# A graph-attention layer on one core: s of the last two pairs of row tiles taken first, the first row of R made on chip, and the check of value ranges made later

## The reference

```python
Wh = X @ W.T
s_i = Wh @ r[:256, 0]
s_j = Wh @ r[256:, 0]
e = s_i[:, None] + s_j[None, :]
e = jnp.where(e >= 0, e, 0.2 * e)
e = jnp.where(A == 0, -jnp.inf, e)
output = jax.nn.softmax(e, axis=1) @ Wh
x = _layernorm(x + gelu(output), axis=-1)
```

## Time and profile before

| | |
|---|---|
| median of 3 runs | 1580.56 us (1579.71 to 1581.5) |
| profiled execution, own time | 1579.36 us |
| its span, first to last instruction | 1577.7 us |
| PE busy | 98% |
| DVE busy | 94% |
| ACT busy | 75% |
| POOL busy | 29% |
| mean granted TensorE clock | 0.992 of 2.4 GHz |

### The profile page before, as it was taken

The page is one execution under the profiler, slowest core; times in us unless marked ns, Lnnn a source line. Parts: engine busy times, 40 slices in busy tenths (PEclk is TensorE's granted clock), DMA queues, the critical chain, the costliest instruction groups (busy, mean ns, idle before and its releaser), DMA issues.

```text
span 1577.7 us, 37073 instructions
## 1 busy us (share of the span) xinstructions
PE 1545.3 (98%) x12685; PEld 1534.9 (97%) x12685; DVE 1483.0 (94%) x1852; ACT 1178.4 (75%) x1527; POOL 455.1 (29%) x660
## 2 busy tenths in 40 slices
PE   8969999999999999999999999999999999999995
PEld 7869999999999999999999999999999999999995
DVE  4789999999999999999999999999999999999995
ACT  5666687777777777877777777777777777777773
POOL 0022223232232323223332322333232233333220
PEclk9989999999999999999999999999999999999998
DMA  7466776968787696878778686877878687787860
GB/s 172 103 92 84 104 104 84 136 79 124 97 118 102 88 131 84 124 92 124 96 95 125 90 122 87 127 94 100 119 95 124 81 127 97 101 115 100 113 93 28
DMA packets 295267, 164.41 MB, mean 104 GB/s; under 512 B 12336, under 2 KB 291120, under 8 KB 295216
## 3 DMA queue, kind: packets, MB, share of 16 engines
q0 software_dynamic: 278976, 142.12, 68.9%
q1 hardware_dynamic: 16240, 21.80, 5.0%
HBM read 289.67 MB, written 8.42 MB: 189 GB/s over the span
## 4 chain that ended last, share of the span: by engine, by line
PE 95%; issue 3%; ACT 1%; DMA 1%; POOL 0%; SPq 0%; POOLq 0%; DVE 0%; ACTq 0%
PE acc L644 30%; PE acc L634 30%; PE acc L637 30%; PE acc L607 3%; PE acc L595 1%; ACT gates L338 0%; DMA Pw<-in_x 0%; DMA R_row<-w_rows 0%; ACT WV_hi L332 0%; ACT P_hi L414 0%; DMA w_rows<-w_in 0%; POOL adj_in L246 0%; POOL rstd L283 0%; SPq L191 0%; POOLq L58 0%
## 5 line engine op out<-in xcount | busy, mean ns | idle before, releaser
L634 PE MATMUL acc<-WV_hi,P_hi 128*128 (+1 forms) x4096 | 999.2, 282 | 8.2 <-ACT P_hi L414 8.1
L637 PE MATMUL acc<-WV_lo,P_hi 128*128 (+1 forms) x4096 | 998.1, 281 | 0.0
L634 PEld LDWEIGHTS acc<-WV_hi,P_hi 128*128 128x128 f32 x4096 | 775.1, 189 | 8.7 <-ACT P_hi L414 8.3
L414 ACT CAST P_hi<-Pw 128x1024 fp32r<-128x1024 f32 x512 | 536.5, 1048 | 317.5 <-DVE Pw L496 160.7
L637 PEld LDWEIGHTS acc<-WV_lo,P_hi 128*128 128x128 f32 x4096 | 772.9, 189 | 0.0
L496 DVE SCALAR_TENSOR_TENSOR Pw<-R_row,X,gatesT 128x512 f32<-128x512 f32 x1024 | 710.3, 746 | 2.6 <-DMA R_row<-w_rows 2.6
L506 DVE TENSOR_TENSOR P_lo<-Pw,P_hi 128x1024 fp32r<-128x1024 f32 x512 | 625.0, 1221 | 40.2 <-ACT P_hi L414 37.4
L246 POOL DMA_DIRECT2D adj_in<-in_adj x512 | 330.4, 654 | 873.5 <-ACT gates L338 819.1
L644 PE MATMUL acc<-WV_hi,P_lo 128*128 (+1 forms) x4096 | 576.2, 283 | 0.0
L338 ACT ACTIVATE gates<-adj_in 128x1024 uint8<-128x1024 bf16 x512 | 536.7, 1048 | 34.6 <-DMA adj_in<-in_adj 25.7
L644 PEld LDWEIGHTS acc<-WV_hi,P_lo 128*128 128x128 f32 x4096 | 527.5, 189 | 0.0
(11 more groups left out here) (60 smaller groups left out, 193.7 us busy)
## 6 DMA issues: line engine op xcount, KB each, us to landing
adj_in<-in_adj POOLq DMA_DIRECT2D x512, 256.0 KB, 5.3
out<-y SPq DMA_DIRECT2D x64, 128.0 KB, 6.0
y<-in_x POOLq DMA_DIRECT2D x60, 128.0 KB, 6.0
Pw<-in_x SPq DMA_DIRECT2D x48, 128.0 KB, 3.7
R_row<-w_rows SPq DMA_DIRECT2D x16, 256.0 KB, 6.6
x_res<-in_x SPq DMA_DIRECT2D x20, 128.0 KB, 2.7
w_in<-in_L_gnn_W SPq DMA_DIRECT2D x1, 256.0 KB, 2.7
w_rows<-w_in SPq DMA_DIRECT2D x1, 32.0 KB, 2.1
```

The costliest lines, as they stand in the source:

```text
L414: nc.scalar.copy(P_hi[:, u % 2], Pw[u][:]).then_inc(s_hi, 1)
L634: nc.tensor.matmul(acc[r_][:, v, 0:HC], P_hi[:, u % 2, par, bass.ts(v, P)], WV_hi[:, k, :], start=(first and u == 0 and par == 0), stop=False)
L637: nc.tensor.matmul(acc[r_][:, v, 0:FOUT], P_hi[:, u % 2, par, bass.ts(v, P)], WV_lo[:, k, :], start=False, stop=False)
```

## The change

1. PE runs `wh_product` only for pairs 0 to 29. For pairs 30 and 31 it first takes the two columns of s alone (`s_product`), then the 256 columns (`late_product`), after all of s is done. `copy_x(31)` goes between the two high parts of pair 29 on ACT.
2. The row 0 of R no longer goes through the memory. DVE multiplies an identity of 32 x 32 by the 16 columns of s that belong to the row (`spread`), one matmul with a matrix of ones puts the sum on all partitions (`ps_row`), DVE cuts it and ACT takes the exponential into `R_row[:, 0]`. The way through w_rows stays for the other rows.
3. The gates of pieces 0 and 1 are made on ACT during pairs 12, 14, ... 26; their loads are issued earlier, those of pieces 2 and 3 during the product, and the transpose of piece 0's gates goes behind pair 27 on DVE.
4. The high parts, low parts and maxima of tiles 60 to 63, and the second and third of the local extrema, move behind the start: on ACT two high parts into the first two groups, on DVE as `late_part` into pieces 1 to 5 of block 0, whose pieces are now written out.
5. The verdict goes to POOL (`verdict`), behind the adjacency loads of block 0. `applies` runs its body at once and waits for the flag at its end, with no branch on it.

```diff
         def applies(eng, body):
+            body()
             eng.wait_ge(s_flag, 1)
-            flag = eng.value_load(taken[0:1, 0:1], min_val=0, max_val=1)
-            with eng.If(flag == 1):
-                body()
...
-            load_rows(0, 0)
-
-            sp.wait_ge(s_Rld[0], 16)
...
+            pool.wait_ge(s_xT, 6)
+            load(0, 0, 0, 0)
             pool.wait_ge(s_xT, 10)
-            load(0, 0, 0, 0)
-            pool.wait_ge(s_xT, 18)
             load(0, 0, 0, 1)
-            pool.wait_ge(s_red, 2)
-            nc.gpsimd.partition_all_reduce(top[:, 0:2], red[:, 0:2], P, REDUCE_MAX).then_inc(s_top, 1)
-            pool.wait_ge(s_red, 3)
-            nc.gpsimd.partition_all_reduce(top[:, 2:3], red[:, 2:3], P, REDUCE_MAX).then_inc(s_top, 1)
+            pool.wait_ge(s_gate, GP)
+            load(0, 0, 1, 0)
+            pool.wait_ge(s_gate, 2 * GP)
+            load(0, 0, 1, 1)
+            pool.wait_ge(s_red, 1)
+            nc.gpsimd.partition_all_reduce(top[:, 0:1], red[:, 0:1], P, REDUCE_MAX).then_inc(s_top, 1)
...
+                def verdict():
+
+                    pool.wait_ge(s_red, 3)
+                    nc.gpsimd.partition_all_reduce(top[:, 1:3], red[:, 1:3], P, REDUCE_MAX).then_inc(s_fit, 1)
+                    pool.wait_ge(s_fit, 1)
+                    nc.gpsimd.tensor_scalar(fits[:, 0:1], top[:, 0:1], top[:, 1:2], MAX_SPREAD, ALU.add, ALU.is_le).then_inc(s_fit, 1)
+                    nc.gpsimd.tensor_scalar(fits[:, 1:3], top[:, 0:2], MAX_S, None, ALU.is_le).then_inc(s_fit, 1)
+                    nc.gpsimd.tensor_scalar(fits[:, 3:4], top[:, 2:3], MAX_WH, None, ALU.is_le).then_inc(s_fit, 1)
+                    pool.wait_ge(s_fit, 4)
+                    for q in range(1, 4):
+                        nc.gpsimd.tensor_tensor(fits[:, 0:1], fits[:, 0:1], fits[:, q:q + 1], ALU.mult).then_inc(s_fit, 1)
+                        pool.wait_ge(s_fit, 4 + q)
+                    nc.gpsimd.tensor_copy(taken[0:1, 0:1], fits[0:1, 0:1]).then_inc(s_flag, 1)
...
+            act.wait_ge(s_rcut, 1)
+            nc.scalar.activation(R_row[:, 0, :], R_row[:, 0, :], ACT.Exp, bias=shift[:], scale=ALPHA - 1.0).then_inc(s_R0, 1)
             act.wait_ge(s_cut, 1)
             nc.scalar.activation(Rc[:].rearrange("p (r m) -> p m r", r=4),
                                  s_i_cut[:].rearrange("p (m r) -> p m r", r=4),
                                  ACT.Exp, bias=shift[:], scale=ALPHA - 1.0).then_inc(s_Rc, 1)
-            nc.scalar.activation(X[:], S[:, :, 1], ACT.Exp, bias=shift[:], scale=1.0 - ALPHA)
+            act.wait_ge(s_wh, NP - 1)
+            late_high_part(NC - 4)
+            late_high_part(NC - 3)
             act.wait_ge(s_Rt, 1)
...
                             nc.scalar.copy(P_hi[:, u % 2], Pw[u][:]).then_inc(s_hi, 1)
+                            if not before and c == 0 and u < 2:
+                                if u == 0:
+                                    act.wait_ge(s_wh, NP)
+                                late_high_part(NC - 2 + u)
...
+            low_part_of(2 * (NP - 3))
+            copy_s(NP - 3)
+            copy_late_s(NP - 2)
+            dve.wait_ge(s_s, NP - 1)
+            row_s = S[0:32, :, 0].rearrange("p (g e) -> p g e", e=4)[:, :, 0:1]
+            nc.vector.tensor_tensor(spread, ident[0:32, 0:32].unsqueeze(1).to_broadcast([32, 16, 32]),
+                                    row_s.to_broadcast([32, 16, 32]), ALU.mult).then_inc(s_dg, 1)
+            copy_late_s(NP - 1)
             dve.wait_ge(s_s, NP)
             nc.vector.tensor_reduce(red[:, 0:1], S[:, :, 1], AX.X, ALU.max).then_inc(s_red, 1)
-            nc.vector.tensor_reduce(red[:, 1:2], S[:, :, 1], AX.X, ALU.min, negate=True).then_inc(s_red, 1)
+            low_part_of(2 * (NP - 3) + 1)
+            wh_maximum(NP - 3)
             dve.wait_ge(s_top, 1)
...
             dve.wait_ge(s_dve, 2)
+            dve.wait_ge(s_row, 1)
+            nc.vector.tensor_scalar(R_row[:, 0, :], ps_row, neg_M[:], None, ALU.max).then_inc(s_rcut, 1)
...
+            def late_part(n):
+
+                if 1 <= n <= 4:
+                    low_part_of(NC - 5 + n)
+                if n == 2 or n == 4:
+                    wh_maximum(NP - 3 + n // 2)
+                if n == 5:
...
-            for j in range(NP):
+            for j in range(NP - 2):
                 wh_product(j)
...
+            s_product(NP - 2)
+            s_product(NP - 1)
+            pe.wait_ge(s_dg, 1)
+            pe.wait_ge(s_const, 3)
+            nc.tensor.matmul(ps_row, ones, spread.rearrange("p g n -> p (g n)"), start=True, stop=True).then_inc(s_row, 1)
+            late_product(NP - 2, 0)
+            late_product(NP - 2, 1).then_inc(s_wh, 1)
+            late_product(NP - 1, 0)
             pe.wait_ge(s_Rc, 1)
-            nc.tensor.transpose(acc[0][0:NC, 0, 0:P], Rc[:], ident[:]).then_inc(s_Rt, 1)
+            nc.tensor.transpose(ps_Rt, Rc[:], ident[:]).then_inc(s_Rt, 1)
+            late_product(NP - 1, 1).then_inc(s_wh, 1)
```

More of the change, by code:

```diff
@@ L109, in narrow_path @@
         ps_wh = [half[:, :, 0:FOUT + 2] for half in (acc[1][:, 0:2], acc[1][:, 2:4], acc[0][:, 2:4])]
+        ones = y[0:32, 0, 0:P]
+        spread = y[0:32, 2:4, :].rearrange("p u (g n) -> p (u g) n", n=32)
+        ps_s = [acc[0][:, j, 0:4] for j in range(2)]
+        ps_row = acc[0][:, 0, :]
+        ps_Rt = acc[0][0:NC, 1, 0:P]
         gate_of = gatesT[:].bitcast(U8).rearrange("p b (i r) -> p b r i", r=4)
@@ L134, in narrow_path @@
         s_flag = sem("flag_ready")
+        s_X = sem("x_factors_ready")
         s_Rc = sem("r_columns_ready")
@@ L298, in block_loads @@
                             scale_bias(t - 1)
-                block_loads(0, 0, first=2, before=False)
+                def verdict():
[10 more added lines that the diff above has]
+                    nc.gpsimd.tensor_copy(taken[0:1, 0:1], fits[0:1, 0:1]).then_inc(s_flag, 1)
+                block_loads(0, 0, first=4, before=False)
+                verdict()
                 block_loads(0, 1)
@@ L322, in copy_x, with high_part @@
                 nc.scalar.copy(xT[:, j % 2, :], ps_xT[j % 2]).then_inc(s_xTc, 1)
-            def high_part(j):
+            def high_part(j, between=None):
                 act.wait_ge(s_wh, j + 1)
@@ L333, in high_part @@
                                          scale=V[:, k:k + 1]).then_inc(s_hi0, 1)
+                    if between and r_ == 0:
+                        between()
             def gate(i, u):
@@ L398, in row_block @@
                     for c in range(PC):
-                        ahead = not (last and c == PC - 1)
+                        ahead = not (last and c == PC - 1) and (before or c > 0)
                         if ahead:
                             act.wait_ge(s_adj[1 - c % 2], 64 * (PC // 2 * t + c // 2) + 64 * (1 + c % 2))
-                            if before or c > 0:
-                                act.wait_ge(s_mask, PC * t + c)
+                            act.wait_ge(s_mask, PC * t + c)
                         for u in range(GP):
@@ L507, in low_part, with piece @@
                                             ALU.subtract).then_inc(s_lo, 1)
-                def piece(ah, r_, cp, i, first=False, den_of=None):
+                def piece(ah, r_, cp, i, first=False, den_of=None, late=False):
                     t = 2 * ah + r_
@@ L521, in piece @@
                             low_part(GP * n + (u - 1), u - 1)
+                        if late and u == 1:
+                            late_part(2 * cp + i)
                         if den_of is not None and u == 1:
@@ L532, in row_block @@
                     e = t - 1 if before else None
-                    dve.wait_ge(s_Rld[r_], 16 * ah + 16)
-                    piece(ah, r_, 0, 0, first=not before, den_of=e)
+                    if not before:
+                        dve.wait_ge(s_R0, 1)
+                        for n in range(PC):
+                            piece(ah, r_, n // 2, n % 2, first=n == 0, late=True)
+                        return
+                    dve.wait_ge(s_Rld[r_], 16 * ah + 16 * r_)
+                    piece(ah, r_, 0, 0, den_of=e)
                     piece(ah, r_, 0, 1)
```

102 lines of the change are left out of this document (66 added, 36 removed).

## The result

The changed kernel takes 1587.02 us (median of 4 runs, 1585.18 to 1590.04), the kernel before 1580.84 in the same set. The ratio is 1.0045, 95% interval 1.0031 to 1.0058: slower by 6.2 us by the medians and 7 by the ratio, where 9 us faster was forecast. On another chip the same kernel gave 1.0023 (1.0011 to 1.0036). The profiled execution has 1585.18 us with a span of 1583.5.

What follows compares the result with a forecast made beforehand. PE was taken to bound the kernel, with a hole of 12.15 us and a half clock before the main part to win. Start 7.7 plus clock 2.6 minus waits 1.3 made 9.0 us: 1580.56 to 1571.6 us, range 1570.0 to 1575.5.

Steps and rivals of the forecast that it cites:

- Seven steps at 0.73 and a reduction are some 5.5 us ... free: Verdict on POOL behind block 0's last load: some 5.5 us, delaying block 1's first load by about 2.5, at no cost.
- a slack of 3.9 us: Block 1's first load: wanted 12 us after the end of piece 5, needs 8.1, which leaves 3.9.
- The prediction's own worst case: Verdict on POOL at 1.4 us a step: it would cost up to 1 us.
- POOL's loads of pieces 2 and 3 are issued before 76 and cost nothing: POOL's adjacency loads during the x product, issued before 76 us: no cost to the start.
- the 7.7 us forecast for the start: Start of the main part: first matmul moves from 92.10 to 84.4 us, 7.7 earlier; range 6.2 to 7.9.
- The clock: Rival: clock falls in the pause before the main part (1572.9 us) or already in the thin stretch (1574.0); chance 0.20.
- the thin stretch: PE's sparse work from 76.3 us: s products, ones, late products; a clock drop there puts the start at about 86.8.
- I expect the full clock throughout: PE around the main part's start: no pause over 1 us, so the half clock's cost of 2.6 us is won.
- Late work on DVE: Block 0, pieces 1 to 5: 3.7 us of late work gives 1.3 us of PE waits; bounds 0 and 3.7.
- The rival on the slower side: Clock drops in the thin stretch and stays at half well into block 0; at six groups 1590 us; chance 0.02.
- colliding x loads: Rival: adjacency loads collide with streaming x, PE waits in some pairs; 1579.6 us, no measurable change; chance 0.03.

Runs made afterwards that it cites:

- e2: The changed kernel with the verdict's comparisons and flag on DVE in piece 7 of block 0, the reduction still on POOL: 1574.61 us, ratio 0.9959.
- e5: The changed kernel again, unchanged, for a second profile: 1581.51 us, ratio 1.0023.
- e11: The kernel of e1 with DVE waiting in piece 5 for the verdict's flag, so at rest during the verdict: 1580.0 us in its one run.
- e6: The kernel of e1 with the first load of row block 1 issued ahead of the verdict, which stays on POOL: 1572.0 us, ratio 0.9962.
- e4: The kernel before, with piece 1's four loads issued behind the transposes of pair 31 instead of pair 17: 1584.35 us, ratio 1.0034.
- e1: The changed kernel with piece 3's four loads moved on POOL behind the global maximum's reduction, verdict still on POOL: 1576.7 us, ratio 0.9979.
- e3: The changed kernel with both edits, of e1 and of e2: 1571.21 us, ratio 0.9942.
- e7: The kernel of e3 with part 2 undone, so row 0 of R goes through the memory again: 1581.34 us, ratio 1.0009.
- e9: The kernel of e3 without the late maxima of |Wh| of pairs 30 and 31: 1570.02 us, ratio 0.9950.
- e10: The kernel of e3 again, unchanged, as the yardstick of its set: 1572.55 us, ratio 0.9958.

## Why the prediction was wrong

**The step that failed** is "Seven steps at 0.73 and a reduction are some 5.5 us ... free", in "Parts 4 and 5". Measured: 19.7 us. Two things were missing. The first is the configuration between a reduction and elementwise work: 7.1 us, with no instruction of its own in the timeline (e2, e5, e11). The second is that POOL's operations last longer while DVE works (e11 against e5). The seven steps and the reduction take 2.1 us when DVE rests, so 0.73 was even high for the work itself. The structure of the step was right (what is queued behind, when it is wanted, a slack of 3.9 us), and e6 points to its place as what counts; the size was wrong by 14 us. The prediction's own worst case was also added up wrongly: with 1.4 us a step the verdict is 10.2 us, delays the load by 7.2, and makes it 3.3 late, not "up to 1 us". The trace of the kernel before has the fact, and the prediction didn't use it:

```profile
POOL n_mean L274 <- issue: 9.1, 1, 9.1
```

That is the first elementwise operation behind the reductions, in a place where nobody waited for it. The next 14 of that line had no such wait.

The Trainium skill, "GPSIMD Engine Reference", "Instruction dispatch", says that the first call of freshly loaded code on this engine costs some 6 us and shows no instruction. The trace agrees in kind, but its steps are longer, 8.0 (e4) and 7.1 us (e5). The Trainium skill, "SBUF — State Buffer", "SBUF: two separate sides", says that an instruction of DVE with two inputs and one of POOL that reads the same memory exclude each other for their whole length. The reduction of 0.37 us in e11 and 0.79 in e5, and the three products of 0.73 and 4.14, agree in kind. The 5.05 us of the first profile are longer than any one instruction of DVE there (1.3 us at most), so there the reduction would have had to lose against several in a row.

Of the 14.8 us between the forecast and the profiled span, this stall is 10.35 (8.3 and 2.05 of half clock), the later start 2.9, the half clock behind it 1.3, a wait in a later block 0.8; the waits for late work came out 1.2 lower. That leaves 0.7 not found.

**The second failed term** is "POOL's loads of pieces 2 and 3 are issued before 76 and cost nothing". They pushed the same kind of step, 8.2 us, behind 74.4 and the reduction from 79.35 to 82.53. That is 2.9 of the 7.7 us forecast for the start. e1 takes the step out of the way: its reduction is at 78.20, its first matmul at 84.79.

**The start, once POOL is out of the way.** 84.4 forecast, 84.47 in e3, where the clock stayed full. The prices of the s products (2.02 for both pairs with the wait between), the spread (0.68 for 0.70), the cut (0.75 for 0.68) and the exponential (0.72 for 0.585) hold.

**The clock** was a rival at 0.20 and came true in the changed kernel in both its forms. In the thin stretch 12 late matmuls take 4.54 us, where they take 2.86 at the full clock of e3, and the clock is at half again from 87.33 to 90.20, behind a wait of PE. "I expect the full clock throughout" therefore failed too, by 1.3 us behind the start. Of the ten profiles with the two-column products the thin stretch has the full clock in four (e2, e3, e6, e11) and not in six (the changed kernel, e1, e5, e7, e9, e10). In the four the products of s begin at 76.33 us or later, in the six at 75.97 or earlier; why this goes together is open. Where it falls, the start comes later: by 1.4 us in e10 against e3, both from V of pair 29.

**Late work on DVE** was priced at 1.3 us of PE waits; e3 shows 0.2 in block 0. A piece takes DVE a little less than the 11.1 us that I added up: in e3 four pieces with their late work take 46.65 us (weights at 92.90 and 139.55), 2.8 of it late work by the starts, so 11.0 a piece. That is some 0.5 us in five pieces; the rest of the difference is not located. So e3's nearness to the forecast is partly a cancelling: start 7.6, clock 2.6 and waits 0.2 would make 10.0 us, the profiled spans differ by 8.0 (1577.7 and 1569.7), and 1.2 of the rest is the wait in a later block, which the forecast had at nothing.

**The rival on the slower side** named the clock. The one that came true was in the list of things called free. Of the others, colliding x loads did not show: PE's busy time in the x product is full (64.00 of 64.00 us from 12 to 76 in the changed kernel).

**Open:** why POOL's waits behind DVE differ so much between executions (0.79 and 5.05 us for the same reduction, 0.37 with DVE at rest). In the changed kernel's profile the two long operations end 0.35 and 0.32 us after DVE went to its transpose (152.65, 163.62), which has one input. That is their length in e11 (0.37 and 0.31), as if they had begun only then. It points to two-input instructions back to back, but no run tried it apart. Open too: why ACT waits for a load in later blocks in some executions (e3, e10) and not in others.

## What to carry to other kernels

Before an operation is moved to an engine, ask what kind of work that engine did last, and look in the trace for its first operation of the new kind: a wait put down to "issue" there is a price, even where it cost nothing. Put such a switch where the engine waits anyway, and ahead of transfers rather than behind them (e1), and issue what others wait for before the slow work (e6). A step called free needs its slack and its worst price side by side: with 3.9 us of slack, a step of three and a half times its price is the whole result.

## What the runs showed of the hardware that I had not expected

- A configuration of POOL takes 8.0 to 8.2 us ahead of its first reduction over partitions and 6.9 to 7.2 us (9.3 in e6) between a reduction and elementwise work. It begins when POOL reaches it in order, and loads issued behind the reduction need none (e1: the loads follow it at once).
- POOL's small operations of 0.2 to 0.4 us took up to 5 us while DVE worked without a pause, and their length changes from run to run.
- A store of 32 KB of 2.1 us took 6.0 us behind 1 MB of loads (e7), and 3.0 to 5.0 us in seven other profiles: it was done 8.2 to 8.5 us after the first of these loads was issued.
- In the stretch of two-column, ones and first late products the granted clock differs from execution to execution: PE is busy 3.70 of 4.00 us from 78 to 82 in both e3 and e10, and the clock is 1.00 in the one and 0.78 in the other.
